# One edit to a fused audio tower on one core: taps and projection of the first image pair by tile, and eps inside the square

## The chip, the cores and the metric

The kernel runs on one core of a Trainium2 chip. The metric is the time of one execution on the device in microseconds. One execution was also recorded by the hardware profiler. Five engines appear in it: TensorE (PE; PEld is its weight load), VectorE (DVE), ScalarE (ACT), GpSimd (POOL), and SyncE (SP), which starts most of the DMAs. Each works through its own list of instructions in order, and semaphores tie the lists together.

## What is computed

The input `x` has 16 images of 64 channels by 250 tokens. Cut to what matters:

```python
x_sp = depthwise_conv(x, conv_w, K=3, pad=1) + conv_b        # (16, 64, 250)
x_mixed = swapaxes(x_sp, 1, 2) @ lin_w.T + lin_b + emb.mean(0)   # (16, 250, 128)
h = (x_mixed - mean) * rsqrt(var + 1e-5) * ln_g + ln_b
n = layernorm(h)
QK = (n @ WQ) @ (n @ WK).T
c0 = argmin(QK[0].sum(-1))
A = softmax(QK / 8); A[:, c0, :] = 0
h = h + A @ (n @ WV)
n = layernorm(h)
h = h + (gelu(n @ tril(W1).T + b1)) @ tril(W2).T + b2        # the FFN mixes along the 128 features
```

Everything is float32, except for the shift of the projection, which pairs 2 to 7 add as three bfloat16 parts.

## The kernel before, in words

Two images form a pair k (0 to 7): channels of one on partitions 0 to 63, of the other on 64 to 127, tokens along the free axis. An image's 250 tokens are split into two tiles of 125, the even ones (a = 0) and the odd ones (a = 1), so a pair has four tiles n = 2 * image + a.

**Front, per pair.** The three taps of the convolution are `first_tap` (ScalarE, line 479; for pair 0 it is `first_tap_0` on VectorE, line 629), `second_tap` and `third_tap` (VectorE, lines 634 and 644), each over 128 x 250. The result is `xc`. TensorE projects it with centred weights `lin_c` and adds the centred shift `cb_all`: `project_0_taps` and `project_0_bias` for pair 0 (lines 287 and 294), `project_1` (301), and `project(k)` for two pairs at a time (313). As weights and shift are centred over the 128 features, a row of the result has mean zero, and its variance is the mean of its squares. `square(k, n)` on ScalarE (line 529) squares a tile, scaled by 128 to the power -0.5, and sums the rows into `var_x`. `root_x` on GpSimd (line 189) raises it to -0.5. For pairs 0 and 1 eps comes in as a 129th column of the projection: `lin_c` has 0 there and `cb_all` has the square root of 128 eps (lines 780 and 781). For pairs 2 to 7 `root_x` adds eps in an operation of its own (line 194). `scale_x` (VectorE, 662) multiplies by this root and by gamma, and `head_h` (VectorE, pairs 0 and 1) or `add_beta` (GpSimd, 216) adds beta. Then `stats_1`, `aggregate_1`, `root_1` and `normalize_1` (or, for pairs 0 and 1, ScalarE's `normalize_tile` and `normalize_1_head`) make the normalized `n1`.

**Attention, per image b.** TensorE: `turn_n1` (349), `queries` (360), `scores` (366), `turn_a` (383), `mix` (395), `attend` (404). ScalarE carries each result out of PSUM: `out_n1t` (557), `out_p` (561), `exps` (567), `out_at` (575), `out_mix` (579). VectorE does `row_max` (709) and the residual. **FFN, per pair j.** `turn_n2`, `up`, `gelu`, `down`, `finish`.

The order of the work on each engine is written out by hand, at the foot of each block: lines 263 to 270 for GpSimd, 448 to 475 for TensorE, 598 to 621 for ScalarE, 785 to 813 for VectorE. `keep_warm` (274) issues multiplications whose results nobody reads. On ScalarE the pieces of the front lie between those of attention: the squares of pairs 2 and 3 are placed from line 601 to 603, those of pair 4 in line 605, of pair 5 in lines 606 and 607. GpSimd's operations have their operands in SBUF alone.

PSUM has eight banks. Pair 0's four tiles lie in `bank_x0` (image 0) and `bank_x1` (image 1). VectorE's first `scale_x(0, 0, 1)` waits for two squares and not one (line 664), since the second square reads the same bank.

Of the kernel before, what the change touches and what calls it, by code (L numbers as in the profile page):

```python
# [5 lines left out]
ALU = mybir.AluOpType  # L6
# [5 lines left out]
EPS = 1e-5  # L12
# [3 lines left out]
def audio_tower(nc, x, tok_pack, weights, rows, out):  # L16
# [4 lines left out]
    E = D + 1  # L21
# [8 lines left out]
    with ExitStack() as ctx:  # L30
# [6 lines left out]
        def bank(name):  # L37
# [5 lines left out]
        x0_ps = [t[0:H, 0:2 * E].rearrange("p (a d) -> p a d", a=2) for t in bank_x]  # L43
        x1_ps = [t[0:H, 0:2 * E].rearrange("p (a d) -> p a d", a=2) for t in bank_s]
# [23 lines left out]
        lin_c = sb("lin_c", [128, E])  # L68
# [3 lines left out]
        cb_all = sb("cb_all", [128, E])  # L72
        cb_all_2 = cb_all[:, :].unsqueeze(1).broadcast_to((128, 2, E))
# [28 lines left out]
        xc = [sb(f"xc{p}", [128, T]) for p in range(CONVS)]  # L102
        xc_halves = [t[:, :].rearrange("c (p a) -> c a p", a=2) for t in xc]
        squared = sb("squared", [H, NP, 4, E])
        var_x = sb("var_x", [H, NP, 4])
        var_x_eps = sb("var_x_eps", [H, NP, 4])
# [34 lines left out]
        ones_ready, iota_ready, tri_ready, mean_w_ready, warm_ready, columns_set = (  # L141
            sem(n) for n in ("ones_ready", "iota_ready", "tri_ready", "mean_w_ready", "warm_ready", "columns_set"))
# [3 lines left out]
        cb_mid_ready, cb_rest2_ready, cb_ready, below_ready, token_sum_ready, xvar_eps_ready = (  # L146
            sem(n) for n in ("cb_mid_ready", "cb_rest2_ready", "cb_ready", "below_ready", "token_sum_ready",
                             "xvar_eps_ready"))
        qk_mm, qk_copied, wv_mm, wv_ready, w1_mm, w1_ready = (
            sem(n) for n in ("qk_mm", "qk_copied", "wv_mm", "wv_ready", "w1_mm", "w1_ready"))  # L150
        tap0_0_ready = sem("tap0_0_ready")
# [121 lines left out]
        def _(pe):  # L273
# [13 lines left out]
            def project_0_taps():  # L287
                pe.wait_ge(lin_centred, 1)
                pe.wait_ge(conv_ready, 1)
                for a in range(2):  # L290
                    for place, half in halves(x0_ps):
                        nc.tensor.matmul(place[:, a, :], xc_halves[0][half, a, :], lin_c[half, :], start=(a == 0), stop=False)

            def project_0_bias():
                pe.wait_ge(row_pick_ready, 2)
                pe.wait_ge(cb_all_ready, 1)
                for place, half in halves(x0_ps):
                    nc.tensor.matmul(place, row_pick[half, 0:1].broadcast_to((C, H)), cb_all_2[half],
                                     start=False, stop=True).then_inc(x_mm, 1)

            def project_1():
                pe.wait_ge(conv_ready, 2)
                for place, half in halves(x1_ps):
                    nc.tensor.matmul(place, row_pick[half, 0:1].broadcast_to((C, H)), cb_all_2[half],
                                     start=True, stop=False)
                for a in range(2):
                    for place, half in halves(x1_ps):
                        last = nc.tensor.matmul(place[:, a, :], xc_halves[1][half, a, :], lin_c[half, :],
                                                start=False, stop=(a == 1))
                        if a == 1:  # L310
                            last.then_inc(x_mm, 1)

            def project(k):
                if k == 2:
                    pe.wait_ge(ones_ready, 1)
                    pe.wait_ge(cb_ready, 1)
                pe.wait_ge(conv_ready, k + 2)
                pe.wait_ge(x_scaled, 4 if k == 2 else 4 * k)
                for place, half in halves(x_two_ps):
                    nc.tensor.matmul(place, ones_b[half, :], cb_rows_4[half], start=True, stop=False)  # L320
                for q in range(2):
                    for a in range(2):
                        for place, half in halves(x_two_ps):
                            last = nc.tensor.matmul(place[:, q, a, :], xc_halves[(k + q) % CONVS][half, a, :], lin_c[half, 0:D],  # L324
                                                    start=False, stop=(q == 1 and a == 1))
                            if q == 1 and a == 1:
                                last.then_inc(x_mm, 1)
# [124 lines left out]
            keep_warm(2)  # L452
            project_0_taps(); project_0_bias()
# [24 lines left out]
        def _(act):  # L478
            def first_tap(k):
                if k == 1:  # L480
                    act.wait_ge(pads_zeroed, 2)
                act.wait_ge(landed_x[k], 16)
                if k >= 2:
                    act.wait_ge(tap01_ready, k - 1)
                nc.scalar.activation(tap0[k % 2][:, :], x_all[:, k, 0:T], ACT.Identity, scale=tok_w[:, D:D + 1],
                                     bias=conv_b).then_inc(tap0_ready, 1)

            def centre_lin():
                nc.scalar.activation(lin_scaled[:, :], lin_t, ACT.Identity, scale=-1.0 / D,
                                     accum_out=neg_lin_mean[:, :]).then_inc(lin_summed, 1)  # L490
                act.wait_ge(lin_summed, 1)
                act.wait_ge(columns_set, 1)
                nc.scalar.activation(lin_c[:, 0:D], lin_t, ACT.Identity, bias=neg_lin_mean[:, :]).then_inc(lin_centred, 1)

            def centre_bias():
# [4 lines left out]
                act.wait_ge(columns_set, 2)  # L500
                nc.scalar.activation(cb_all[:, 0:D], cb_ps, ACT.Identity, bias=neg_cb_mean[:, :]).then_inc(cb_all_ready, 1)

            def bias_hi():
                act.wait_ge(cb_all_ready, 1)
                nc.scalar.activation(cb_hi[:, :], cb_all[:, 0:D], ACT.Copy).then_inc(cb_hi_ready, 1)
# [122 lines left out]
        def _(dve):  # L628
            def first_tap_0():
                dve.wait_ge(landed_x[0], 16)  # L630
                nc.vector.tensor_scalar(tap0[0][:, :], x_all[:, 0, 0:T], tok_w[:, D:D + 1], conv_b,
                                        ALU.mult, ALU.add).then_inc(tap0_0_ready, 1)

            def second_tap(k):
                if k == 0:
                    dve.wait_ge(tap0_0_ready, 1)
                else:
                    dve.wait_ge(tap0_ready, k)
                if k >= 2:
                    dve.wait_ge(conv_ready, k - 1)  # L640
# [21 lines left out]
            def scale_x(k, first, m):  # L662
                dve.wait_ge(rstd_x_ready, 4 * k + first + m)
                if k == 0 and first + m == 1:
                    dve.wait_ge(xvar_ready, 2)
# [4 lines left out]
                for n in range(first, first + m):  # L670
                    x = (x0_ps, x1_ps)[k][n // 2][:, n % 2, 0:D] if k < 2 else x_two_ps[n // 2][:, k % 2, n % 2, :]
# [108 lines left out]
            nc.vector.memset(lin_c[:, D:E], 0.0).then_inc(columns_set, 1)  # L780
            nc.vector.memset(cb_all[:, D:E], (EPS * D) ** 0.5).then_inc(columns_set, 1)
# [3 lines left out]
            first_tap_0(); second_tap(0); third_tap(0); bias_rest(); second_tap(1); bias_rest2()  # L785
            third_tap(1)
# [55 lines left out]
```

## Time and profile before

| | |
|---|---|
| time, median of 3 runs | 94.32 us (94.21 to 94.5) |
| the profiled execution | 93.75 us; its span in the trace 92.0 us |
| TensorE (PE) busy | 85.0 us, 92% of the span, 541 instructions |
| VectorE busy | 73.6 us, 80%, 283 |
| ScalarE busy | 67.6 us, 73%, 241 |
| GpSimd busy | 54.9 us, 60%, 89 |
| granted TensorE clock | full in all 40 slices of the span |

Busy shares are means over stages with different limits: the front of the first pairs fills roughly the first 18 us, attention and the later pairs' fronts overlap until about 70, then comes the FFN. A row of the chain of waits has start, duration, engine and line, in time order. A row of the timeline has start, duration, engine, line, operation, output and inputs, shapes and how many instructions are merged in it; in brackets is the idle time before it and what ended it. Ends of matmuls are modelled, so consecutive groups on PE overlap slightly.

### The profile page before, as it was taken

The numbers are of one execution on the slowest core, as the hardware profiler recorded it, in microseconds if no ns is written. First come the engines' busy times: TensorE is split into PE (matmuls) and PEld (weight loads), VectorE is DVE, ScalarE is ACT, GpSimd is POOL, SyncE is SP. The second block draws the span as 40 slices with busy tenths as digits, with TensorE's granted clock in tenths as the row PEclk, the third lists the DMA queues.
The fourth block names the chain that finished last, engine by engine and source line by source line (L and its number), as shares of the span: only waits on it lengthen the run. The fifth ranks groups of instructions, "written<-read, shape, count | busy, mean of one in ns | idle before, by whom it ended". The sixth has DMA issues, their size and how long they took to land.

```text
span 92.0 us, 1984 instructions
## 1 busy us (share of the span) xinstructions
PE 85.0 (92%) x541; PEld 69.5 (76%) x541; DVE 73.6 (80%) x283; ACT 67.6 (73%) x241; POOL 54.9 (60%) x89
## 2 busy tenths in 40 slices
PE   5979987699999999999999999999999999999940
PEld 2446565379799989999899899989887988687730
DVE  2259999998999998999998899869769395862560
ACT  1688999999999769969787988666796735555400
POOL 5508768898856793999982079972708437460000
PEclk9999999999999999999999999999999999999999
DMA  1986000000000000000000000000000003425364
GB/s 23 218 289 200 0 0 4 4 0 0 11 0 0 0 0 0 0 7 4 4 0 0 0 0 7 0 0 0 0 0 0 0 7 111 115 69 154 108 188 150
DMA packets 3828, 3.84 MB, mean 42 GB/s; under 512 B 413, under 2 KB 3690, under 8 KB 3818
## 3 DMA queue, kind: packets, MB, share of 16 engines
q1 hardware_dynamic: 3466, 3.35, 13.1%
q10 hardware_dynamic: 352, 0.38, 1.4%
q8 instruction: 4, 0.07, 0.3%
q14 instruction: 6, 0.05, 0.2%
HBM read 1.68 MB, written 2.05 MB: 40 GB/s over the span
## 4 chain that ended last, share of the span: by engine, by line
PE 72%; DVE 8%; POOL 8%; DMA 3%; issue 3%; ACT 1%; POOLq 0%; DVEq 0%
PE bank_m L400 14%; PE bank_s L373 12%; PE bank_o L411 8%; PE bank_s L431 7%; PE bank_at L391 7%; PE bank_np L364 6%; PE bank_np L444 4%; PE bank_x L422 4%; POOL rstd L207 4%; DMA tok_w<-tok_dram 3%; PE bank_np L356 3%; PE bank_at L444 3%; POOL rstd_x L198 2%; DVE hb_all L774 2%; DVE bn L688 1%
## 5 line engine op out<-in xcount | busy, mean ns | idle before, releaser
L373 PE MATMUL bank_s<-n1t,pt 128*125 128x250 f32 x64 | 16.0, 375 | 0.5 <-ACT pt L565 0.5
L400 PE MATMUL bank_m<-at,n 125*128 125x250 f32 x64 | 16.2, 374 | 0.0
L570 ACT ACTIVATE a<-bank_s,neg_max 125x250 f32<-125x250 f32 x32 | 15.1, 479 | 0.7 <-DVE neg_max L711 0.7
L222 POOL TENSOR_TENSOR hb_all<-h_all,rows_sb 125x512 f32<-125x512 f32 x8 | 10.2, 1272 | 4.0 <-DVE h_all L747 4.0
L711 DVE TENSOR_REDUCE neg_max<-bank_s 125x2 f32<-125x500 f32 x16 | 10.7, 670 | 2.1 <-PE bank_s L373 2.1
L373 PEld LDWEIGHTS bank_s<-n1t,pt 128*125 128x125 f32 x64 | 11.0, 187 | 1.6 <-issue 0.6
L400 PEld LDWEIGHTS bank_m<-at,n 125*128 125x128 f32 x64 | 11.2, 190 | 0.9
L577 ACT ACTIVATE at<-bank_at 125x500 f32<-125x500 f32 x16 | 9.6, 597 | 1.9 <-PE bank_at L391 1.9
L207 POOL TENSOR_TENSOR rstd<-var_eps,neg_half 125x4 f32<-125x4 f32 (+2 forms) x11 | 9.5, 863 | 1.9 <-DVE var_eps L700 0.6
L364 PE MATMUL bank_np<-n1t,qk_w 128*128 128x250 f32 x32 | 9.6, 381 | 0.6 <-ACT n1t L559 0.6
L747 DVE SCALAR_TENSOR_TENSOR h_all<-bank_o,rinv_keep,h_all 125x128 f32<-125x128 f32 x32 | 9.6, 343 | 0.2
L391 PE MATMUL bank_at<-ident,a 125*125 125x125 f32 x64 | 9.7, 274 | 0.0
L411 PE MATMUL bank_o<-wv_c,mixed 128*125 128x128 f32 x64 | 9.6, 272 | 0.0
L411 PEld LDWEIGHTS bank_o<-wv_c,mixed 128*125 128x125 f32 x64 | 8.9, 187 | 0.8 <-issue 0.5
L391 PEld LDWEIGHTS bank_at<-ident,a 125*125 125x125 f32 x64 | 8.8, 188 | 0.9 <-issue 0.2
L214 POOL TENSOR_TENSOR rstd<-var_eps,neg_half 125x4 f32<-125x4 f32 x8 | 8.8, 1105 | 0.6
L565 ACT ACTIVATE pt<-bank_np 128x250 f32<-128x250 f32 x16 | 6.2, 385 | 3.2 <-PE bank_np L364 3.0
L581 ACT ACTIVATE mixed<-bank_m 128x250 f32<-128x250 f32 x16 | 6.1, 383 | 3.2 <-PE bank_m L400 3.2
L537 ACT ACTIVATE squared<-bank_x 125x128 f32<-125x128 f32 (+1 forms) x28 | 7.7, 293 | 0.9 <-PE bank_x L324 0.9
L218 POOL TENSOR_TENSOR h_all<-scaled,rows_sb 125x512 f32<-125x512 f32 x6 | 7.7, 1290 | 1.0 <-DVE scaled L672 1.0
L593 ACT ACTIVATE g<-bank_s,w_sb 128x500 f32<-128x500 f32 x8 | 5.3, 676 | 3.9 <-PE bank_s L431 3.3
L431 PE MATMUL bank_s<-n2t,w_c 128*128 128x500 f32 x16 | 8.0, 583 | 0.0
(121 smaller groups left out, 193.4 us busy)
## 6 DMA issues: line engine op xcount, KB each, us to landing
out_dram<-hb_all SPq DMA_DIRECT2D x7, 224.0 KB
x_all<-x_dram SPq DMA_DIRECT2D x8, 125.0 KB, 4.9
w_sb<-weights_dram SPq DMA_DIRECT2D x1, 320.5 KB, 5.7
out_dram<-hb_all SPq DMA_DIRECT2D x2, 112.0 KB
rows_sb<-rows_dram ACTq DMA_DIRECT2D x1, 187.5 KB
out_dram<-hb_all SPq DMA_DIRECT2D x6, 26.0 KB
tok_w<-tok_dram ACTq DMA_DIRECT2D x1, 130.0 KB, 3.1
out_dram<-hb_all ACTq DMA_DIRECT2D x2, 26.0 KB
```

Source lines behind the costliest of these rows:

```text
L207: pool.tensor_tensor(rstd1[:, k, tiles], var1_eps[:, k, tiles], neg_half[:, tiles], ALU.pow)\
L222: pool.tensor_tensor(hb_all[:, j, :, :], h_tiles[:, j, :, :], b2_4, ALU.add).then_inc(hb_ready, 1)
L364: nc.tensor.matmul(p_ps, qk_w[:, :], n1t[b % DEEP][:, :], start=True, stop=True).then_inc(p_mm, 1)
L373: last = nc.tensor.matmul(s_ps[b % 2][:, a, :], pt[b % DEEP][:, a * H:(a + 1) * H], n1t[b % DEEP][:, :], start=True, stop=True)
L391: last = nc.tensor.transpose(at_ps[:, c, a * H:(a + 1) * H], a_sb[b % DEEP][:, a, c * H:(c + 1) * H], ident[0:H, 0:H])
L400: last = nc.tensor.matmul(mix_ps, n1[b // 2 % (HELD // 2)][:, 2 * (b % 2) + c, :], at_sb[b % DEEP][:, c, :], start=(c == 0), stop=(c == 1))
L411: last = nc.tensor.matmul(o_ps[:, a, :], mixed[b % DEEP][:, a * H:(a + 1) * H], wv_c[:, :], start=True, stop=True)
L431: nc.tensor.matmul(f1_ps[j % 2], w1_c[:, :], n2t[j % 2][:, :], start=True, stop=True).then_inc(f1_mm, 1)
L570: ins = nc.scalar.activation(a_sb[b % DEEP][:, a, :], s_ps[b % 2][:, a, :], ACT.Exp, bias=neg_max[b % 2][:, a:a + 1], accum_out=exp_sum[:, ...
L577: nc.scalar.activation(at_sb[b % DEEP][:, :, :], at_ps, ACT.Copy).then_inc(at_ready, 1)
L711: nc.vector.tensor_reduce(neg_max[b % 2][:, :], s_ps[b % 2], AX_X, ALU.max, negate=True).then_inc(max_ready, 1)
L747: last = nc.vector.scalar_tensor_tensor(h, o_ps[:, a, :], rinv_keep[:, b // 2, n:n + 1], h, ALU.mult, ALU.add)
```

## The change

Five things are done.

1. `square` adds `root_eps`, a column of 125 partitions with the value (eps / 128) to the power 0.5, inside the square, for all pairs. The sum over a row of (x / sqrt(128) + sqrt(eps / 128)) squared is the variance plus eps, since the row's sum is zero.
2. With that the 129th column goes (`E = D + 1` becomes D all over) with its two memsets, and so do the six additions of eps in `root_x`. One memset of `root_eps` comes instead.
3. The three taps of pair 0 are done tile by tile: six VectorE operations over 128 x 125, which read `x_all` at every second element and write `xc` at every second one.
4. The projection of pair 0 is done tile by tile: taps and bias of tile a = 0 of both images, then those of a = 1. Tile (image 0, a = 1) gets a place in `bank_o`, so the two tiles of image 0 lie in banks of their own. `x_mm` rises after (image 0, a = 0), (image 0, a = 1) and (image 1, a = 1). The shift is added by four multiplications of 128 columns, before by two of 258. The wait of `scale_x(0, 0, 1)` for the second square goes. `w1_centre`, which uses `bank_o`, waits for two tiles of `x_scaled`.
5. One of the two `keep_warm` multiplications ahead of the projection of pair 0 goes.

The lists are otherwise in the same order. The diff, cut to its core (renumbered semaphore counts and the declarations are left out):

```diff
-        x0_ps = [t[0:H, 0:2 * E].rearrange("p (a d) -> p a d", a=2) for t in bank_x]
+        x0_ps = [[bank_x[0][0:H, 0:D], bank_o[0:H, 0:D]], [bank_x[1][0:H, 0:D], bank_x[1][0:H, D:2 * D]]]
...
             def root_x(k, first, m):
                 tiles, done = slice(first, first + m), 4 * k + first + m
                 pool.wait_ge(xvar_ready, done)
-                var = var_x
-                if k >= 2:
-                    pool.tensor_tensor(var_x_eps[:, k, tiles], var_x[:, k, tiles], eps[:, tiles], ALU.add)\
-                        .then_inc(xvar_eps_ready, 1)
-                    pool.wait_ge(xvar_eps_ready, k - 1)
-                    var = var_x_eps
-                pool.tensor_tensor(rstd_x[:, k, tiles], var[:, k, tiles], neg_half[:, tiles], ALU.pow).then_inc(rstd_x_ready, m)
+                pool.tensor_tensor(rstd_x[:, k, tiles], var_x[:, k, tiles], neg_half[:, tiles], ALU.pow).then_inc(rstd_x_ready, m)
...
-            def project_0_taps():
-                pe.wait_ge(lin_centred, 1)
+            def project_0_taps(a):
+                if a == 0:
+                    pe.wait_ge(lin_centred, 1)
+                pe.wait_ge(conv_0_ready, a + 1)
+                for par in range(2):
+                    half = slice(par * C, (par + 1) * C)
+                    nc.tensor.matmul(x0_ps[par][a], xc_halves[0][half, a, :], lin_c[half, :], start=True, stop=False)
+
+            def project_0_bias(a):
+                if a == 0:
+                    pe.wait_ge(row_pick_ready, 2)
+                    pe.wait_ge(cb_all_ready, 1)
+                for par in range(2):
+                    half = slice(par * C, (par + 1) * C)
+                    last = nc.tensor.matmul(x0_ps[par][a], row_pick[half, 0:1].broadcast_to((C, H)), cb_all[half, :],
+                                            start=False, stop=True)
+                    if par == 0 or a == 1:
+                        last.then_inc(x_mm, 1)
...
             def w1_centre():
                 pe.wait_ge(tri_ready, 2)
+                pe.wait_ge(x_scaled, 2)
                 nc.tensor.matmul(w1_ps, centre[:, :], w1_t, start=True, stop=True).then_inc(w1_mm, 1)
...
             bias_mean()
-            keep_warm(2)
-            project_0_taps(); project_0_bias()
+            keep_warm(1)
+            project_0_taps(0); project_0_bias(0); project_0_taps(1); project_0_bias(1)
             keep_warm(4)
...
             def square(k, n):
                 par, a = n // 2, n % 2
-                if k < 2:
-                    act.wait_ge(x_mm, 2 * k + par + 1)
-                    x, junk = (x0_ps, x1_ps)[k][par][:, a, :], squared[:, k, n, :]
+                if k == 0:
+                    act.wait_ge(root_eps_set, 1)
+                    act.wait_ge(x_mm, min(n + 1, 3))
+                    x = x0_ps[par][a]
+                elif k == 1:
+                    act.wait_ge(x_mm, 3 + par + 1)
+                    x = x1_ps[par][:, a, :]
                 else:
-                    act.wait_ge(x_mm, 4 + 2 * (k // 2 - 1) + par + 1)
-                    x, junk = x_two_ps[par][:, k % 2, a, :], squared[:, k, n, 0:D]
-                nc.scalar.activation(junk, x, ACT.Square, scale=float(D) ** -0.5,
+                    act.wait_ge(x_mm, 5 + 2 * (k // 2 - 1) + par + 1)
+                    x = x_two_ps[par][:, k % 2, a, :]
+                nc.scalar.activation(squared[:, k, n, :], x, ACT.Square, scale=float(D) ** -0.5, bias=root_eps[:, :],
                                      accum_out=var_x[:, k, n:n + 1]).then_inc(xvar_ready, 1)
...
-            def first_tap_0():
-                dve.wait_ge(landed_x[0], 16)
-                nc.vector.tensor_scalar(tap0[0][:, :], x_all[:, 0, 0:T], tok_w[:, D:D + 1], conv_b,
+            def x0_shifted(c):
+                return x_all[:, 0, c:c + T - 1:2]
+
+            def first_tap_0(a):
+                if a == 0:
+                    dve.wait_ge(landed_x[0], 16)
+                nc.vector.tensor_scalar(tap0_halves[:, a, :], x0_shifted(a), tok_w[:, D:D + 1], conv_b,
                                         ALU.mult, ALU.add).then_inc(tap0_0_ready, 1)
 
+            def second_tap_0(a):
+                dve.wait_ge(tap0_0_ready, a + 1)
+                nc.vector.scalar_tensor_tensor(tap01_halves[:, a, :], x0_shifted(a + 1), tok_w[:, D + 1:D + 2],
+                                               tap0_halves[:, a, :], ALU.mult, ALU.add).then_inc(tap01_0_ready, 1)
+
+            def third_tap_0(a):
+                dve.wait_ge(tap01_0_ready, a + 1)
+                nc.vector.scalar_tensor_tensor(xc_halves[0][:, a, :], x0_shifted(a + 2), tok_w[:, D + 2:D + 3],
+                                               tap01_halves[:, a, :], ALU.mult, ALU.add).then_inc(conv_0_ready, 1)
+
...
             def scale_x(k, first, m):
                 dve.wait_ge(rstd_x_ready, 4 * k + first + m)
-                if k == 0 and first + m == 1:
-                    dve.wait_ge(xvar_ready, 2)
...
-            nc.vector.memset(lin_c[:, D:E], 0.0).then_inc(columns_set, 1)
-            nc.vector.memset(cb_all[:, D:E], (EPS * D) ** 0.5).then_inc(columns_set, 1)
+            nc.vector.memset(root_eps[:, :], (EPS / D) ** 0.5).then_inc(root_eps_set, 1)
             nc.vector.memset(ones_b[:, :], 1.0).then_inc(ones_ready, 1)
             dve.wait_ge(pads_zeroed, 2)
             dve.wait_ge(landed_tok, 16)
-            first_tap_0(); second_tap(0); third_tap(0); bias_rest(); second_tap(1); bias_rest2()
-            third_tap(1)
+            first_tap_0(0); second_tap_0(0); third_tap_0(0); first_tap_0(1); second_tap_0(1)
+            third_tap_0(1); bias_rest(); second_tap(1); bias_rest2(); third_tap(1)
```

## Rows read from the trace of the kernel before

**Rows 1.** Chain of waits: start us, duration us, engine, line

```profile
24.17 0.70 DVE n L706
...
24.92 0.43 PE bank_np L356 x2
...
26.62 0.85 PE bank_m L400 x4
```

**Rows 2.** Busy time by stretch: us, then PE, PEld, DVE, ACT, POOL

```profile
9.20:18.30 9.10, 7.44 (x45) 4.86 (x44) 8.91 (x37) 8.92 (x44) 7.08 (x15) 1.00 0.01 2
24.92:87.40 62.48, 62.48 (x403) 54.66 (x403) 52.46 (x206) 46.39 (x151) 37.22 (x45) 1.00 0.08 22
```

**Rows 3.** Waits of PE from 9 to 18.5: total us, times, longest

```profile
PE bank_np L364 <- ACT n1t L559: 0.6, 1, 0.6
```

**Rows 4.** Timeline of PE: start us, duration us

```profile
6.09 0.63 PE L298 MATMUL bank_x<-cb_all,row_pick 64*125 64x258 f32 x4
...
20.55 0.43 PE L320 MATMUL bank_x<-cb_rows,ones_b 64*125 64x512 bf16 x2
...
23.80 1.01 PE L400 MATMUL bank_m<-at,n 125*128 125x250 f32 x4
...
26.04 0.58 PE L364 MATMUL bank_np<-n1t,qk_w 128*128 128x250 f32 x2
...
29.23 0.59 PE L364 MATMUL bank_np<-n1t,qk_w 128*128 128x250 f32 x2
...
38.60 0.59 PE L364 MATMUL bank_np<-n1t,qk_w 128*128 128x250 f32 x2
```

**Rows 5.** Timeline of ACT: start us, duration us

```profile
6.09 0.59 ACT L485 ACTIVATE tap<-x_all,tok_w 128x250 f32<-128x250 f32 x1 [0.36 <-DMA x_all<-x_dram]
...
9.24 0.28 ACT L537 ACTIVATE squared<-bank_s 125x129 f32<-125x129 f32 x1 [0.32 <-PE bank_s L308]
...
17.87 0.38 ACT L565 ACTIVATE pt<-bank_np 128x250 f32<-128x250 f32 x1
...
20.11 0.69 ACT L549 ACTIVATE n<-h_all,rstd 125x128 f32<-125x128 f32 x2 [0.21 <-POOL rstd L207]
...
25.39 0.38 ACT L559 ACTIVATE n1t<-bank_np 128x250 f32<-128x250 f32 x1
...
28.34 0.45 ACT L559 ACTIVATE n1t<-bank_np 128x250 f32<-128x250 f32 x1
...
37.95 0.39 ACT L559 ACTIVATE n1t<-bank_np 128x250 f32<-128x250 f32 x1
```

**Rows 6.** Groups of ACT by shape: count, busy us, mean ns, idle before

```profile
L570 ACT ACTIVATE a<-bank_s,neg_max 125x250 f32<-125x250 f32 x32 | 15.1, 479 | 0.7 <-DVE neg_max L711 0.7
...
L537 ACT ACTIVATE squared<-bank_x 125x128 f32<-125x128 f32 x24 | 6.7, 298 | 0.9 <-PE bank_x L324 0.9
...
L565 ACT ACTIVATE pt<-bank_np 128x250 f32<-128x250 f32 x16 | 6.2, 385 | 3.2 <-PE bank_np L364 3.0
...
L537 ACT ACTIVATE squared<-bank_x 125x129 f32<-125x129 f32 x4 | 1.0, 264 | 0.0
...
L501 ACT ACTIVATE cb_all<-bank_s,neg_cb_mean 128x128 f32<-128x128 f32 x1 | 0.4, 368 | 0.0
```

**Rows 7.** Timeline of DVE: start us, duration us

```profile
3.96 0.41 DVE L631 TENSOR_SCALAR tap<-x_all,tok_w 128x250 f32<-128x250 f32 x1 [2.33 <-DMA tok_w<-tok_dram]
...
4.92 0.48 DVE L648 SCALAR_TENSOR_TENSOR xc<-x_all,tok_w,tap 128x250 f32<-128x250 f32 x1
5.83 0.35 DVE L654 SCALAR_TENSOR_TENSOR cb_rest<-cb_hi,neg_below,cb_all 128x128 f32<-128x128 bf16 x1 [0.43 <-ACT cb_hi L505]
...
18.28 2.12 DVE L672 SCALAR_TENSOR_TENSOR scaled<-bank_x,rstd_x,rows_sb 125x128 f32<-125x128 f32 x8
...
21.35 0.87 DVE L688 BATCH_NORM_STATS2 bn<-h_all 125x6 f32<-125x128 f32 x4 [0.36 <-POOL h_all L218]
```

**Rows 8.** Instructions of line 194, POOL: duration ns min/median/max

```profile
L194 POOL TENSOR_TENSOR var_x_eps<-var_x,eps x6: 202/224/748, 16.2 to 42.7; 125x4 f32<-125x4 f32 x6
```

More of the change, by code:

```diff
@@ L71, in audio_tower @@
         mean_w = sb("mean_w", [128, 128])
-        cb_all = sb("cb_all", [128, E])
-        cb_all_2 = cb_all[:, :].unsqueeze(1).broadcast_to((128, 2, E))
+        cb_all = sb("cb_all", [128, D])
+        cb_all_2 = cb_all[:, :].unsqueeze(1).broadcast_to((128, 2, D))
         cb_hi, cb_mid, cb_rows = (sb(n, [128, D], BF16) for n in ("cb_hi", "cb_mid", "cb_rows"))
@@ L102, in audio_tower @@
         xc = [sb(f"xc{p}", [128, T]) for p in range(CONVS)]
+        tap0_halves, tap01_halves = (t[0][:, :].rearrange("c (a p) -> c a p", a=2) for t in (tap0, tap01))
         xc_halves = [t[:, :].rearrange("c (p a) -> c a p", a=2) for t in xc]
-        squared = sb("squared", [H, NP, 4, E])
+        squared = sb("squared", [H, NP, 4, D])
+        root_eps = sb("root_eps", [H, 1])
         var_x = sb("var_x", [H, NP, 4])
-        var_x_eps = sb("var_x_eps", [H, NP, 4])
         rstd_x = sb("rstd_x", [H, NP, 4])
@@ L140, in audio_tower @@
                              "row_pick_zeroed", "row_pick_ready"))
-        ones_ready, iota_ready, tri_ready, mean_w_ready, warm_ready, columns_set = (
-            sem(n) for n in ("ones_ready", "iota_ready", "tri_ready", "mean_w_ready", "warm_ready", "columns_set"))
+        ones_ready, iota_ready, tri_ready, mean_w_ready, warm_ready, root_eps_set = (
+            sem(n) for n in ("ones_ready", "iota_ready", "tri_ready", "mean_w_ready", "warm_ready", "root_eps_set"))
         lin_summed, lin_centred, cb_mm, cb_summed, cb_all_ready, cb_hi_ready, cb_rest_ready = (
@@ L285, in halves, with project_1 @@
                 return [(place[par], slice(par * C, (par + 1) * C)) for par in range(2)]
-            def project_0_taps():
-                pe.wait_ge(lin_centred, 1)
-                pe.wait_ge(conv_ready, 1)
[L290 to L302, printed above, removed]
+            def project_0_taps(a):
[15 more added lines that the diff above has]
+                        last.then_inc(x_mm, 1)
+            def project_1():
+                pe.wait_ge(conv_ready, 1)
                 for place, half in halves(x1_ps):
@@ L323, in project @@
                         for place, half in halves(x_two_ps):
-                            last = nc.tensor.matmul(place[:, q, a, :], xc_halves[(k + q) % CONVS][half, a, :], lin_c[half, 0:D],
+                            last = nc.tensor.matmul(place[:, q, a, :], xc_halves[(k + q) % CONVS][half, a, :], lin_c[half, :],
                                                     start=False, stop=(q == 1 and a == 1))
@@ L482, in first_tap @@
                 act.wait_ge(landed_x[k], 16)
[L483 to L484 removed]
+                if k == 2:
+                    act.wait_ge(tap01_0_ready, 2)
+                elif k >= 3:
+                    act.wait_ge(tap01_ready, k - 2)
                 nc.scalar.activation(tap0[k % 2][:, :], x_all[:, k, 0:T], ACT.Identity, scale=tok_w[:, D:D + 1],
@@ L491, in centre_lin @@
                 act.wait_ge(lin_summed, 1)
-                act.wait_ge(columns_set, 1)
-                nc.scalar.activation(lin_c[:, 0:D], lin_t, ACT.Identity, bias=neg_lin_mean[:, :]).then_inc(lin_centred, 1)
+                nc.scalar.activation(lin_c[:, :], lin_t, ACT.Identity, bias=neg_lin_mean[:, :]).then_inc(lin_centred, 1)
             def centre_bias():
@@ L499, in centre_bias @@
                 act.wait_ge(cb_summed, 1)
-                act.wait_ge(columns_set, 2)
-                nc.scalar.activation(cb_all[:, 0:D], cb_ps, ACT.Identity, bias=neg_cb_mean[:, :]).then_inc(cb_all_ready, 1)
+                nc.scalar.activation(cb_all[:, :], cb_ps, ACT.Identity, bias=neg_cb_mean[:, :]).then_inc(cb_all_ready, 1)
             def bias_hi():
                 act.wait_ge(cb_all_ready, 1)
-                nc.scalar.activation(cb_hi[:, :], cb_all[:, 0:D], ACT.Copy).then_inc(cb_hi_ready, 1)
+                nc.scalar.activation(cb_hi[:, :], cb_all[:, :], ACT.Copy).then_inc(cb_hi_ready, 1)
             def bias_mid():
@@ L653, in bias_rest @@
                 dve.wait_ge(cb_hi_ready, 1)
-                nc.vector.scalar_tensor_tensor(cb_rest[:, :], cb_hi[:, :], neg_below[0][:, :], cb_all[:, 0:D],
+                nc.vector.scalar_tensor_tensor(cb_rest[:, :], cb_hi[:, :], neg_below[0][:, :], cb_all[:, :],
                                                ALU.mult, ALU.add).then_inc(cb_rest_ready, 1)
```

31 lines of the change are left out of this document (14 added, 17 removed).

## The prediction

> **What bounds the kernel now.** I read the chain of waits first. It ends in one long stretch of TensorE: VectorE's normalization for pair 2 runs 24.17 to 24.87, TensorE starts image 4 at 24.92, and the chain doesn't leave TensorE until the last stores [rows 1]. The table of stretches says how dense that is: from 24.92 to 87.40 TensorE is busy 62.48 of 62.48 us [rows 2]. So the end of the kernel is the moment at which TensorE's solid stretch begins, plus 62.5 us that the change doesn't touch, plus any new hole that it tears in it.
>
> What sets the beginning? The same table for 9.20 to 18.30 shows TensorE at 7.44 of 9.10 us, ScalarE at 8.92 and VectorE at 8.91 [rows 2]. The view of waits lists what TensorE waited for there, and ScalarE ended each of it; the longest is 0.6 us for `n1t` [rows 3]. The reader is to see that in this stretch TensorE waits for ScalarE, and ScalarE waits for nothing. Its last idle piece is 0.32 us before the first square of pair 1 at 9.24; then it works without a hole until `out_p(1)` ends at 18.25 [rows 5], and TensorE goes on right behind it. The printed chain runs through GpSimd and VectorE instead, but has little room: the work ahead of image 4 on TensorE, four passes of `mix(0)` from 23.80 that take 0.85 to issue, would let it start at 24.65 [rows 1, 4]. The two routes differ by 0.27 us. A gain on the printed one is capped there; a loss on ScalarE's is paid nearly in full.
>
> **The change, part by part.**
>
> *eps inside the square.* All 32 squares get `bias=root_eps[:, :]`, a [125,1] operand in SBUF, where they had none. The algebra holds because a centred row sums to zero. The operand's price is the step on which the forecast rests. The trace has no square with such an operand, so I bound it by neighbours, all from PSUM. An exponential over 250 elements with a column as bias takes 479 ns, a copy over 250 without one 385: 94 apart. Over 128 elements, `cb_all` with a column takes 368 and the present squares 298: 70 apart [rows 6]. Lower bound 70 ns, and as upper bound 368 less 264 of the cheapest squares, 104 [rows 6]. Below nothing I exclude, since no row with a column is shorter than its like without. I take 94, from 32 and 16 instances. Dependent pieces follow one another closely on ScalarE, so I count it in full.
>
> The Trainium skill, ScalarE: Activation LUTs, section "What ACT_TABLE_LOAD costs", speaks against this change: each per-partition pointer operand adds about 93 ns to an ACTIVATE. By that rule the sum below is the same within 0.03 us, by the lowest row it is 0.5 us smaller. The same section has ACTIVATEs that overlap by about as much, which is why the rival in which nothing is paid is named below.
>
> *GpSimd's additions.* Six `var_x_eps` additions go, 224 ns median each and some 0.13 of waiting behind each [rows 8]: about 0.7 us ahead of `add_beta(2)`. VectorE waited 0.36 for that at 21.35 [rows 7]. VectorE frees at 20.99, so the gain is 0.36 on that route, and 0.27 on TensorE by the cap above. It is worth that only if ScalarE isn't later.
>
> *Taps of pair 0 by tile.* Three operations of 250 elements become six of 125. Before, the third ended at 5.40 (4.92 plus 0.48) [rows 7]. A 128-element form takes 0.35 [rows 7]. Tile 0 from 3.96 [rows 7]: 0.35, 0.35, 0.35 and two steps of 0.035 give 5.08, 0.32 earlier. Tile 1 follows: its first operation starts at about 5.00, and the same chain ends at 6.13, 0.73 later than before. The elements are now two apart; if that made a half cost as much as a whole, 0.48, tile 1 would end at about 6.8. I take the unstrided price and keep the other for the range. Behind it `bias_rest` moves from 5.83 to 6.05 and ends at 6.4, before ScalarE wants it at about 6.6, behind the tap of pair 1 that waited for its DMA until 6.09 and takes 0.59 [rows 5, 7]. Without that cover it would cost 0.2.
>
> Nobody gains from the early tile: ScalarE reaches the first square only at about 6.8, after that same tap, and the old bias product was complete at 6.72 [rows 4, 5]. The dropped wait of `scale_x(0, 0, 1)` is worth nothing for the same reason: VectorE waits for GpSimd's root of tile 0. TensorE finishes later. The bias pair took 0.63, of which 0.09 is drain; half of 0.54 goes to each tile's taps and each tile's bias. So 6.13, 0.15 to start and twice 0.27 give 6.82, against 6.09 plus 0.54, 6.63 (next start 6.65). That is +0.17 for what is queued behind: warm-up products, `qk_product`, `project_1`. One warm-up product less lies before the taps, in idle time: nothing. `project_1` then ends at 9.38. ScalarE, held 0.38 by pair 0's four squares, is free at 8.92 plus 0.38, 9.30. So the first square of pair 1 starts 0.17 late, at 9.41, and covers both.
>
> *Edits with one answer.* 129 columns become 128, one memset goes, `w1_centre` waits for `x_scaled` 2 (met 5 us earlier): nothing. The waits of `first_tap(2)` and `second_tap(2)` on the new semaphores are met by 6.2, 2 us ahead of their instructions: nothing.
>
> **The sum.**
> - Up to `out_p(1)`: 0.17 plus the twelve squares of pairs 1 to 3, 1.13: +1.30, for TensorE behind it too.
> - From there to 24.92 TensorE has slack that absorbs: about 0.22 before `project(4)` at 20.55, which waits for `scale_x(3)` to end at 20.40, 0.06 of small holes, and the 0.27 [rows 4, 7]. Image 4 starts +0.75.
> - ScalarE itself: 1.30 less the 0.21 it had waited for GpSimd at 20.11, plus 0.38 for pair 4's squares: +1.47. Its `out_n1t(4)`, 25.39 plus 0.38, ends at 27.24, and `queries(4)`, due at 26.04, starts 0.22 short of that shift: +1.25 [rows 4, 5].
> - Pair 5's squares: ScalarE +1.85 at `out_n1t(5)`, 28.34 plus 0.45; `queries(5)` at 29.23 has 0.39 of slack: +1.46 [rows 4, 5].
> - ScalarE then has idle time before pair 6 (it is busy 46.39 of 62.48 us [rows 2]) and falls back in step. Seven squares of pairs 6 and 7 stand ahead of `out_n1t(8)`, 0.66, less 0.1 of holes; that copy ended at 38.34 and `queries(8)` started at 38.60 [rows 4, 5]. About 0.2 of slack (0.05 is transit) leaves +0.35, of which I count 0.25, for holes under 0.15 us that no view lists.
>
> Total +1.7. Against the profiled execution's own 93.75 (span 92.0, 1.75 around it) that is 95.45. The median of the runs shown is 94.32, 0.57 above it, and the forecast is for the median: **96.0**.
>
> **The rivals.**
> 1. *Only the head counts.* ScalarE's slack swallows pairs 4 to 7, as its 46.39 of 62.48 us in the last stretch suggests [rows 2]. Then +0.75 remains, 95.1. Against it: the two copies named have 0.27 and 0.44 us of slack. Chance 0.15.
> 2. *Faster: GpSimd's route decides.* The column's 0.1 us hides in ScalarE's overlap between instructions. Then squares cost nothing, ScalarE is 0.17 late at 9.41, which the 0.28 of holes before 23.80 absorbs, and the removed additions bring 0.27: 94.05. It decides once a square costs less than about 0.03 us. Against it: the 94 ns between two groups that follow one another equally closely. Chance 0.07.
> 3. *The two cancel.* A square costs 0.03 to 0.05 and the gain is eaten: 94.3. Chance 0.06.
> 4. *Strided taps are dear.* Tile 1 is done 0.65 later still; `project_1` and ScalarE behind it move by about as much: 96.6. For it: no row has two-apart operands. Against: one element per step seems to be VectorE's pace already (0.13 for 122 elements more). Chance 0.12.
>
> **How the numbers follow.** The likeliest case has 0.60; its own range, from 70 to 104 ns a square, is 95.4 to 96.4. Taking in rival 1 below and rival 4 above, 94.9 to 96.8 leaves some 0.2 out. A measurement here tells 0.3%, 0.28 us, from no change. Rival 2 lies on that edge, half of it under: faster 0.06. Rival 3 and the rest: same 0.07. Slower: 0.87.
>
> **What would show it.** Squares of 125x128 at about 390 ns instead of 298, 32 of them; ScalarE's busy time up by 3 us. The first square of pair 1 at about 9.4, `out_p(1)` near 19.2 instead of 17.87, image 4 near 25.7. New idle time on TensorE between 9 and 30, ended by `n1t`. GpSimd without the additions, and no wait of VectorE for `h_all` at 21. Half taps of 0.35; 0.45 would speak for rival 4. I am wrong if the squares keep their 298 ns, or if they take 390 and TensorE's solid stretch still begins by 25.0: then ScalarE had room where I saw none.

## The result, and the profile after

The changed kernel takes 95.75 us (median of 4 runs, 95.32 to 96.94) against 94.26 for the kernel before (median of 4, 94.21 to 94.5). The ratio is 1.0137, with a 95% interval of 1.009 to 1.0185: slower by 1.3 us. The forecast was 96.0, with 94.9 to 96.8 as range. The profiled execution took 95.55 us, with a span of 93.8. Ratios leave disturbed executions out, here the one of 96.94 us (the median of the other three is 95.55), which is why an interval can be narrower than the spread of its runs.

The groups of ScalarE by shape hold the largest term, against [rows 6]:

```profile
L573 ACT ACTIVATE a<-bank_s,neg_max 125x250 f32<-125x250 f32 x32 | 15.6, 493 | 0.7 <-DVE neg_max L725 0.7
L540 ACT ACTIVATE squared<-bank_x,root_eps 125x128 f32<-125x128 f32 x27 | 10.3, 394 | 0.9 <-PE bank_x L322 0.9
...
L540 ACT ACTIVATE squared<-bank_s,root_eps 125x128 f32<-125x128 f32 x4 | 1.5, 365 | 0.3 <-PE bank_s L306 0.3
```

The name `root_eps` now stands among the inputs, and a square takes 394 ns where it took 298: 96 more, with 94 forecast. The page's first part says what that is over 32 squares, ScalarE from 67.6 to 70.2 us; GpSimd falls from 54.9 to 53.0, as its six additions are gone:

```profile
PE 86.1 (92%) x544; PEld 69.6 (74%) x544; DVE 74.6 (79%) x285; ACT 70.2 (75%) x241; POOL 53.0 (56%) x83
```

The timeline of ScalarE, against [rows 5]:

```profile
5.92 0.60 ACT L486 ACTIVATE tap<-x_all,tok_w 128x250 f32<-128x250 f32 x1 [0.35 <-DMA x_all<-x_dram]
...
9.46 0.37 ACT L540 ACTIVATE squared<-bank_s,root_eps 125x128 f32<-125x128 f32 x1 [0.32 <-PE bank_s L306]
...
19.17 0.38 ACT L568 ACTIVATE pt<-bank_np 128x250 f32<-128x250 f32 x1
...
25.62 0.40 ACT L568 ACTIVATE pt<-bank_np 128x250 f32<-128x250 f32 x1
26.80 0.42 ACT L562 ACTIVATE n1t<-bank_np 128x250 f32<-128x250 f32 x1
```

The first square of pair 1 starts at 9.46 (9.41 forecast), `out_p(1)` at 19.17, 1.30 late (1.30 forecast), `out_n1t(4)` at 26.80, 1.41 late (1.47). The idle piece that stood before 20.11 is gone. Whether the longer squares delay what follows them is seen at the second square of pair 1. Before, it starts 0.26 behind the first (9.24), and in the changed kernel 0.36 behind it (9.46):

```profile
9.50 0.27 ACT L537 ACTIVATE squared<-bank_s 125x129 f32<-125x129 f32 x1
...
9.82 0.36 ACT L540 ACTIVATE squared<-bank_s,root_eps 125x128 f32<-125x128 f32 x1
```

The timeline of VectorE has the third tap of each of pair 0's two tiles, 0.35 us over 125 elements two apart, against [rows 7]:

```profile
4.57 0.35 DVE L648 SCALAR_TENSOR_TENSOR xc<-x_all,tok_w,tap 128x125 f32<-128x125 f32 x1
...
5.60 0.35 DVE L648 SCALAR_TENSOR_TENSOR xc<-x_all,tok_w,tap 128x125 f32<-128x125 f32 x1
```

The timeline of TensorE from its first long wait on, against [rows 4]:

```profile
18.45 0.69 PE L363 MATMUL bank_np<-n1t,qk_w 128*128 128x250 f32 x2 [0.89 <-ACT n1t L562]
...
26.16 0.40 PE L355 MATMUL bank_np<-ident,n 125*128 125x125 f32 x2 [0.16 <-ACT pt L568]
...
27.27 0.69 PE L363 MATMUL bank_np<-n1t,qk_w 128*128 128x250 f32 x2
...
30.65 0.69 PE L363 MATMUL bank_np<-n1t,qk_w 128*128 128x250 f32 x2
...
40.59 0.69 PE L363 MATMUL bank_np<-n1t,qk_w 128*128 128x250 f32 x2
```

`queries(4)` is 1.23 late (1.25 forecast), `queries(5)` 1.42 (1.46), `queries(8)` 1.99 (1.7). The table of stretches gives TensorE more idle time ahead of its solid stretch (6.79 busy of 9.10 us, before 7.44). The solid stretch itself starts 1.24 later and is also longer, 63.30 us for the same 403 instructions that took 62.48 [rows 2]:

```profile
9.20:18.30 9.10, 6.79 (x44) 4.24 (x42) 8.35 (x33) 8.73 (x40) 6.73 (x13) 1.00 0.01 2
26.16:89.46 63.30, 63.30 (x403) 54.40 (x403) 52.32 (x204) 47.51 (x152) 35.48 (x42) 1.00 0.07 21
```

That both rows read fully busy, though one took 0.82 longer, fits the modelled ends of matmuls, which can cover short stops. The chain of waits has such stops at `queries`, which waits for ScalarE's copy `n1t`. For image 4 this copy now ends at 27.22 and `queries` starts at 27.27; before it was 25.77 and 26.04. `queries` takes 0.42 us of the chain in the kernel before:

```profile
26.20 0.42 PE bank_np L364 x2
```

and in the changed kernel, for images 4, 5 and 8:

```profile
27.41 0.55 PE bank_np L363 x2
...
30.74 0.60 PE bank_np L363 x2
...
40.64 0.65 PE bank_np L363 x2
```

Ahead of that the chain has changed hands. It now leads through squares, where it led through GpSimd and VectorE [rows 1]. At its start it has the load of the weights, `w_sb`, for whose landing TensorE waits 0.18 us before `qk_product` at 7.88; this matters below:

```profile
1.72 6.03 DMA w_sb<-weights_dram
...
14.39 1.14 ACT squared L540 x6
15.80 0.70 ACT squared L540 x4
16.50 0.58 ACT n L552 x2
17.07 1.05 ACT squared L540 x6
...
23.77 1.01 ACT squared L540 x5
24.80 0.47 ACT squared L540 x2
```

### The profile page after: what moved, and what is told of

Read it like the earlier page. It is cut to its first block, busy times and chain, and to the rows that moved or that the text cites. A ratio compares the mean times of both kernels' runs of the same rounds, so it can differ in the third digit from the quotient of the medians.

```text
span 93.8 us, 1989 instructions
## 1 busy us (share of the span) xinstructions
PE 86.1 (92%) x544; PEld 69.6 (74%) x544; DVE 74.6 (79%) x285; ACT 70.2 (75%) x241; POOL 53.0 (56%) x83
## 4 chain that ended last, share of the span: by engine, by line
PE 76%; ACT 8%; DMA 6%; DVE 4%; issue 1%; SPq 1%; DVEq 0%
PE bank_m L399 14%; PE bank_s L372 13%; PE bank_o L410 7%; PE bank_np L363 7%; PE bank_at L390 7%; PE bank_s L430 7%; DMA w_sb<-weights_dram 6%; ACT squared L540 5%; PE bank_np L355 4%; PE bank_np L443 4%; PE bank_x L421 4%; PE bank_x L322 3%; PE bank_at L443 3%; DVE hb_all L788 1%; PE bank_x L318 1%
## 5 line engine op out<-in xcount | busy, mean ns | idle before, releaser
L573 ACT ACTIVATE a<-bank_s,neg_max 125x250 f32<-125x250 f32 x32 | 15.6, 493 | 0.7 <-DVE neg_max L725 0.7
L191 POOL TENSOR_TENSOR rstd_x<-var_x,neg_half 125x4 f32<-125x4 f32 (+2 forms) x11 | 10.1, 924 | 8.1 <-ACT squared L540 8.1
L540 ACT ACTIVATE squared<-bank_x,root_eps 125x128 f32<-125x128 f32 x27 | 10.3, 394 | 0.9 <-PE bank_x L322 0.9
L686 DVE SCALAR_TENSOR_TENSOR scaled<-bank_x,rstd_x,rows_sb 125x128 f32<-125x128 f32 x27 | 7.5, 340 | 0.9 <-ACT squared L540 0.7
```

Of the source, the lines that this page charges most:

```text
L191: pool.tensor_tensor(rstd_x[:, k, tiles], var_x[:, k, tiles], neg_half[:, tiles], ALU.pow).then_inc(rstd_x_ready, m)
L540: nc.scalar.activation(squared[:, k, n, :], x, ACT.Square, scale=float(D) ** -0.5, bias=root_eps[:, :], accum_out=var_x[:, k, n:n + 1]).th ...
L573: ins = nc.scalar.activation(a_sb[b % DEEP][:, a, :], s_ps[b % 2][:, a, :], ACT.Exp, bias=neg_max[b % 2][:, a:a + 1], accum_out=exp_sum[:, ...
```

## The experiments

**Which part costs: the column or the tiles?** Four kernels cross the two. The first takes the column out of the changed kernel (ScalarE's group is shown behind the result):

```diff
-                nc.scalar.activation(squared[:, k, n, :], x, ACT.Square, scale=float(D) ** -0.5, bias=root_eps[:, :],
+                nc.scalar.activation(squared[:, k, n, :], x, ACT.Square, scale=float(D) ** -0.5, bias=(EPS / D) ** 0.5,
```

> The changed kernel with one edit: the squares' bias is a number in the instruction and not a column in SBUF. Theory (the column's price on ScalarE's path is the whole loss): squares of 125x128 back from 394 to about 298 ns, the first square of pair 1 at about 9.4, out_p(1) near 18.0, time 94.0 (93.8 to 94.3), as GpSimd's removed additions can now bring up to 0.27 and pair 0's tiles take up to 0.17. Rival (tiling pair 0 delays TensorE and with it all): stays above 95.2.

Measured: 94.15 us, ratio to the kernel before 0.9969 (0.9946 to 0.9992).

```profile
L540 ACT ACTIVATE squared<-bank_x 125x128 f32<-125x128 f32 x27 | 7.7, 300 | 1.0 <-PE bank_x L322 0.9
```

The square is back at 300 ns, and the rival about tiles falls: with the tiles in and the column out, the whole loss is gone. From ScalarE's timeline of this kernel: the first square of pair 1 starts at 9.47, against 9.46 with the column, but `out_p(1)` at 18.15, against 19.17:

```profile
9.47 0.28 ACT L540 ACTIVATE squared<-bank_s 125x128 f32<-125x128 f32 x1 [0.32 <-PE bank_s L306]
...
18.15 0.38 ACT L568 ACTIVATE pt<-bank_np 128x250 f32<-128x250 f32 x1
```

The second puts the column alone into the kernel before (its 129th column and GpSimd's additions out, taps and projection of pair 0 untouched):

```diff
-                nc.scalar.activation(junk, x, ACT.Square, scale=float(D) ** -0.5,
+                nc.scalar.activation(junk, x, ACT.Square, scale=float(D) ** -0.5, bias=root_eps[:, :],
```

> The kernel before with the column alone: eps inside the square as a column, no 129th column, no additions of GpSimd; taps and projection of pair 0, the warm-up and the wait for the second square as before. Theory: 95.5 (95.2 to 95.8), squares at 390 ns; within 0.2 of the changed kernel. Rival (pair 0's tiles are the cause): 94.3.

Measured: 95.65 us, ratio 1.0137 (1.0105 to 1.0168), the changed kernel's own. The third is the same with the number in place of the column.

> The kernel before with eps inside the square as a number in the instruction, no 129th column and no additions of GpSimd; pair 0 as before. Theory: squares at 298 ns, VectorE's wait for h_all at 21 gone, time 94.0, up to 0.27 below the kernel before and not more, since TensorE's own work ahead of image 4 ends at 24.65. Rival (GpSimd's additions were hidden): 94.3, as before.

Measured: 93.67 us, ratio 0.9934 (0.9909 to 0.9958). It beats both kernels: 0.6 us under the one before, 1.9 under the changed one. Against `old_col`, from which it differs in the operand of the squares alone, it is 2.0 us faster: that is the column's price with nothing else changed. VectorE's wait for `h_all` is gone, as expected. The gain over the kernel before is larger than the 0.27 that theory allowed, and the profile doesn't show where it lies: `queries(8)` starts at 38.59, in the profile of before at 38.60 [rows 4], though that profile was a quick execution (below). Two more kernels price the additions. One has tiles, the number for pairs 0 and 1, and GpSimd's additions for the others:

```diff
+                if k >= 2:
+                    pool.tensor_tensor(var_x_eps[:, k, tiles], var_x[:, k, tiles], eps[:, tiles], ALU.add)\
+                        .then_inc(xvar_eps_ready, 1)
```

> Pair 0 by tile as in the changed kernel, eps as a number in the squares of pairs 0 and 1, and GpSimd's six additions for pairs 2 to 7 back. Theory: squares at 298 ns, pair 0's tiles cost TensorE 0.17 at 9.2 and ScalarE as much, most of it absorbed or paid behind the GpSimd route: 94.3 to 94.5. Against tiles_imm this prices the additions (0.2 to 0.3 less there). Rival (tiles are a gain): below 94.1.

Measured: 94.36 us, ratio 1.001 (0.9991 to 1.0029); against 0.9969 that makes the additions worth 0.4 us. The other is the kernel before without the additions and with nothing in their place.

> The kernel before without GpSimd's six additions and nothing else changed. It leaves eps out for pairs 2 to 7. Theory (capped by TensorE's own work ahead of image 4): 0.1 to 0.3 under the kernel before, 94.0 to 94.2. Rival (the whole gain of old_imm, 0.6, is the additions'): 93.7.

Measured: 93.97 us, ratio 0.997 (0.9953 to 0.9987): 0.3 us. The cap of 0.27 is within the uncertainty of both. The rest of `old_imm`'s 0.6, some 0.3, is not clear of noise (its interval and that of `no_adds` overlap). It could belong to the 129th column and its two memsets, but no run isolates them, and the traces don't speak for it: from the first square of pair 1 to `queries(8)` pass 29.33 us in `old_imm` and 29.21 in `no_adds`, which has the 129th column. It stays open. The tiles (with the dropped warm-up product), `tiles_imm` against `old_imm`, cost 0.0035 or 0.3 us with the number, where the two intervals overlap as well, and nothing that can be told with the column (1.0137 both).

**Where does ScalarE's time count?** The changed kernel with the column for one half of the pairs and the number for the other:

```diff
-                nc.scalar.activation(squared[:, k, n, :], x, ACT.Square, scale=float(D) ** -0.5, bias=root_eps[:, :],
+                nc.scalar.activation(squared[:, k, n, :], x, ACT.Square, scale=float(D) ** -0.5,
+                                     bias=root_eps[:, :] if k < 4 else (EPS / D) ** 0.5,
```

> The changed kernel with the column in the squares of pairs 0 to 3 alone; pairs 4 to 7 take the number. Theory (every square that stands ahead of a late copy on ScalarE pays): image 4 on TensorE near 25.8 as in the changed kernel, no further loss later: 0.8 to 1.1 over the kernel with the number everywhere (94.15), so 95.0 to 95.25. Rival (only the head counts): as the changed kernel, 95.7.

> The changed kernel with the column in the squares of pairs 4 to 7 alone; pairs 0 to 3 take the number. Theory: queries(4) 0.2 to 0.35 late, queries(5) 0.3 more, queries(8) 0.3 more: 0.6 to 1.0 over 94.15, so 94.75 to 95.15, and the two halves together give the changed kernel's 1.6. Rival (only the head counts, ScalarE's idle time after 30 us swallows these): 94.15.

Measured: 94.73 (ratio 1.0038, 1.0016 to 1.006) and 94.93 (1.007, 1.0047 to 1.0093). Against 0.9969 the halves cost 0.0069 and 0.0101, or 0.65 and 0.95 us, together 0.0170; the changed kernel's step over `tiles_imm` is 0.0168. The later half is within what was expected, the head below its 0.8 to 1.1. The rival that only the head counts falls: the later half costs about as much. TensorE's timeline of `col_head`, `queries(4)` and `queries(8)`:

```profile
27.03 0.69 PE L363 MATMUL bank_np<-n1t,qk_w 128*128 128x250 f32 x2
...
39.70 0.59 PE L363 MATMUL bank_np<-n1t,qk_w 128*128 128x250 f32 x2
```

and of `col_late`:

```profile
26.41 0.68 PE L363 MATMUL bank_np<-n1t,qk_w 128*128 128x250 f32 x2
...
39.72 0.69 PE L363 MATMUL bank_np<-n1t,qk_w 128*128 128x250 f32 x2
```

In `tiles_imm` the same two start at 26.07 and 38.73. With the column in the head 0.96 is lost by `queries(4)` (0.11 of it already stands at the first square of pair 1, 9.58 against 9.47), and 0.97 by `queries(8)`: nothing more. With the column in the late pairs it is 0.34 and then 0.99. So pairs 4 to 7 lose 0.65 between these two points in a stretch where ScalarE has idle time on the whole. The chain of `col_late` has the same short stops as the changed kernel: `queries` takes 0.60 at 29.86 and 0.65 at 39.77, where an undelayed one takes 0.42. So ScalarE's idle pieces lie elsewhere than the copies for which TensorE stops.

**Twice the suspected cost.** The scale goes in as a second column:

```diff
-                nc.scalar.activation(squared[:, k, n, :], x, ACT.Square, scale=float(D) ** -0.5, bias=root_eps[:, :],
+                nc.scalar.activation(squared[:, k, n, :], x, ACT.Square, scale=root_d[:, :], bias=root_eps[:, :],
```

> The changed kernel with the scale of all squares as a second column of SBUF (same value). Theory (each column operand costs ScalarE about 94 ns and the slack is used up already): squares at about 487 ns, time 97.3 to 97.9. Rival (the first operand is dear, a second one is free, or the loss saturates): below 96.2.

Measured: 100.38 us, median of four between 98.3 and 101.07, no ratio. The operand behaves as expected, 480 ns, 86 more:

```profile
L541 ACT ACTIVATE squared<-bank_x,root_eps,root_d 125x128 f32<-125x128 f32 x27 | 12.7, 480 | 0.9 <-PE bank_x L323 0.9
```

The time doesn't: 4.6 us over the changed kernel where 1.6 to 2.2 were expected. The table of stretches of its profiled execution (us, then PE, PEld, DVE, ACT, POOL busy, the granted clock, the DMA share and GB/s) shows the rest:

```profile
17.00:18.00 1.00, 0.71 (x4) 0.30 (x4) 0.39 (x2) 1.00 (x5) 1.00 (x2) 1.00 0.00 0
18.00:19.00 1.00, 0.35 (x2) 0.11 (x2) 1.00 (x4) 1.00 (x6) 0.19 (x1) 0.85 0.02 8
19.00:20.00 1.00, 0.49 (x1) 0.50 (x2) 1.00 (x6) 1.00 (x6) 0.68 (x1) 0.50 0.00 0
...
25.00:26.00 1.00, 1.00 (x11) 0.74 (x12) 0.86 (x7) 0.75 (x4) 0.20 (x1) 0.74 0.00 0
26.00:27.00 1.00, 1.00 (x17) 0.88 (x14) 0.42 (x1) 0.62 (x4) 0.98 (x1) 1.00 0.00 0
```

TensorE's timeline of the same execution:

```profile
16.55 1.08 PE L373 MATMUL bank_s<-n1t,pt 128*125 128x250 f32 x4 [1.04 <-ACT pt L569]
17.91 0.43 PE L356 MATMUL bank_np<-ident,n 125*128 125x125 f32 x2 [0.29 <-ACT n L553]
19.50 1.20 PE L364 MATMUL bank_np<-n1t,qk_w 128*128 128x250 f32 x2 [1.16 <-ACT n1t L563]
...
21.75 1.87 PE L373 MATMUL bank_s<-n1t,pt 128*125 128x250 f32 x4
```

TensorE waits 1.04, 0.29 and 1.16 us within four microseconds. About 0.4 us into the third wait, at 18.7, the granted clock falls to 0.50, its lower level of 1.2 GHz, and it stays there until 25.5. Four passes of `scores` take 1.87 us there and 1.08 at 16.55. To part the two causes I filled the idle time with work for nothing. It is legal since `bank_at` is free between `out_wv` and `turn_a(0)`:

```diff
+            def keep_warm_at(count):
+                pe.wait_ge(wv_ready, 1)
+                for _ in range(count):
+                    nc.tensor.matmul(bank_at[0:64, :], warm[:, :], warm[:, :].unsqueeze(1).broadcast_to((128, 8, 64)),
+                                     start=True, stop=True)
...
-            turn_n1_tile(0); turn_n1_tile(1); project(2); queries(0); w1_centre(); scores(0); turn_n1(1)
-            queries(1); row_sums(); turn_n1(2); scores(1); turn_a(0); queries(2); project(4); turn_n1(3)
+            turn_n1_tile(0); turn_n1_tile(1); project(2); queries(0); w1_centre(); keep_warm_at(3); scores(0); keep_warm_at(1); turn_n1(1)
+            keep_warm_at(4); queries(1); row_sums(); turn_n1(2); scores(1); turn_a(0); queries(2); project(4); turn_n1(3)
```

> The kernel with two columns (100.38) and eight more multiplications whose results nobody reads, placed on TensorE where it idles between 15 and 19.5 us. Theory (of the 4.6 us between one column and two, some 1.7 are ScalarE's and some 3 are TensorE at the lower of its two levels from 18.9 to 25.3 us): granted clock 0.99 or more, four passes of scores(1) back from 1.87 to about 1.0, time 97.2 to 97.9, although work was added. Rival (the loss is ScalarE's alone, the clock goes with it): 100 or more.

Measured: 98.58 us, ratio 1.0447 (1.0412 to 1.0482), granted clock 0.991 to 0.996 in four of four. Its table of stretches:

```profile
14.00:19.00 5.00, 4.73 (x34) 2.93 (x31) 4.32 (x17) 4.97 (x22) 3.12 (x5) 1.00 0.02 5
19.00:25.00 6.00, 5.68 (x41) 4.17 (x40) 5.53 (x25) 5.90 (x23) 4.85 (x7) 1.00 0.01 1
```

and, from its timeline, the four passes that took 1.87:

```profile
21.30 1.01 PE L379 MATMUL bank_s<-n1t,pt 128*125 128x250 f32 x4
```

The median is 1.8 us lower with eight multiplications more. Three of `col_two`'s four executions had a mean clock of 0.966 to 0.983, and the one at 0.992 took 98.3, as `two_warm` does. So of the 4.6 us some 1.8 are the clock and 2.8 to 3.0 the operand, which is above the 97.2 to 97.9 expected. My size for the operand, 1.7, was too low. 32 squares at 86 ns are 2.8: that fits a second column paid in full, the slack having been used up by the first.

**How far two executions differ.** The kernel before, unchanged, once more.

> The kernel before once more, for a second profile of it: the first one took 93.75, 0.57 under the median. Theory (the difference between executions lies in when the loads land): tok_w, the x of pair 1 or w_sb land 0.1 to 0.4 us later than in the first profile and everything after is shifted by as much. Rival: the front is the same to 0.05 us and the difference lies in the last stores.

Measured: 94.25 us, first square of pair 1 at 9.73 and not 9.24. Two of the three loads named weren't late: VectorE's first tap, behind `tok_w`, starts at 3.82 against 3.96, and the tap of pair 1 at 5.80 against 6.09. The third was. TensorE's timeline of the execution of [rows 4] has:

```profile
4.01 0.46 PE L282 MATMUL bank_s<-tok_w,mean_w 128*128 128x128 f32 x2
...
7.63 0.49 PE L332 MATMUL bank_m<-w_sb 128*128 128x128 f32 x2
```

and that of this one:

```profile
3.95 0.80 PE L282 MATMUL bank_s<-tok_w,mean_w 128*128 128x128 f32 x2
...
8.16 0.46 PE L332 MATMUL bank_m<-w_sb 128*128 128x128 f32 x2 [0.22 <-DMA w_sb<-weights_dram]
```

Two things differ here: the product of shift and means takes 0.80 us where it took 0.46, and `qk_product` waits for `w_sb`. The other profiles part them. Here are four of the kernels with the time that the profile gives `w_sb` from issue to landing, and the starts of `qk_product` and of the first square of pair 1:

| | product at 4.0 | `w_sb` lands | `qk_product` | first square of pair 1 |
|---|---|---|---|---|
| `before` | 0.46 | 5.7 us | 7.63 | 9.24 |
| `old_imm` | 0.80 | 5.8 us | 7.68 | 9.26 |
| `before_2` | 0.80 | 6.3 us | 8.16 | 9.73 |
| `two_warm` | 0.46 | 6.3 us | 8.15 | 9.73 |

The square follows `w_sb` and not the slow product. In all twelve profiles it starts 1.57 to 1.61 us after `qk_product`, and a later landing never goes with an earlier square. So the theory holds for one load, `w_sb`, at 0.6 us and not 0.1 to 0.4. The 0.5 us of the front go through to the end (93.75 and 94.25).

## Why the prediction was right

- *The stretch that sets the start.* TensorE waits for ScalarE, and ScalarE for nothing: shown. Without the column `out_p(1)` moves from 19.17 to 18.15, with the first square of pair 1 in the same place (9.46 and 9.47), and the loss is gone. One wait of TensorE in the changed kernel, 0.77 us before `scores(0)`, is put down to VectorE's `scaled`, which ended at 15.88; ScalarE's copy `pt`, which it needs too, had ended 0.08 before. In `old_col` the same wait is `pt`'s.
- *94 ns a square, of 70 to 104.* Measured 96 (394 less 298), and 94 against `tiles_imm` (300). An exponential and a copy over 250 elements gave it, which differ in their function as well, so that it came this close is in part luck; the nearer shape, `cb_all`, would have given 70. By the rule of the Trainium skill, ScalarE: Activation LUTs, "What ACT_TABLE_LOAD costs", each pointer operand adds about 93 ns; this case's rows agree, 96 for the first and 86 for the second.
- *Nothing hides it.* The second square of pair 1 starts 0.36 behind the first and not 0.26, in `col_two` 0.45: the operand isn't covered by the overlap between instructions. `out_p(1)`, `queries(4)` and `queries(5)` came within 0.05 us of the working.
- *The first square of pair 1, +0.17: the number was luck.* It came at 9.46, 0.22 late, but the four warm-up products behind pair 0's projection start at 6.65 in both profiles. What held `qk_product`, and with it `project_1` and the square, is the wait for `w_sb` (6.0 us to landing against 5.7), which differs between executions of one kernel and which the working didn't have. Measured from the square on, `out_p(1)` is 1.08 late (1.13 forecast) and `queries(8)` 1.77 (1.53).
- *Image 4, +0.75: wrong.* One wait was left out. TensorE started it 1.24 late, because `turn_n1(4)` also waits for `out_p(3)` (25.62 plus 0.40), which I hadn't listed. It made no difference to the sum, as `queries(4)` was to be held for the same shift by `out_n1t(4)`.
- *Pairs 6 and 7, 0.25.* Too small: from `queries(5)` to `queries(8)` the lateness grew from 1.42 to 1.99, by 0.57. In the times the whole step is smaller, 1.3 us by the ratio, in `old_col` too, so the sum of 1.7 was high by 0.4 there. The profiles of before and after are 1.8 apart, but that of before is an execution in which `w_sb` landed early, 0.5 under the second one. Against the median of all four, 95.75, the forecast of 96.0 is 0.25 high, and against 95.55 it is 0.45; both lie inside the range.
- *GpSimd's additions, up to 0.27 and worth nothing behind the column.* Shown by `tiles_adds` and `no_adds`: 0.3 to 0.4 without the column. That with the column the gain is covered is argued from the chain; no run has the column and the additions.
- *Tiles, 0.17 late on TensorE, nothing gained.* The half taps took 0.35, as assumed, so elements two apart cost VectorE nothing that shows, and rival 4 falls. TensorE's tile 1 started 0.40 after VectorE's last tap had started, at 6.00. From VectorE's first tap to the warm-up products behind the projection pass 2.85 us (3.80 to 6.65), before 2.69 (3.96 to 6.65): 0.16 more, as worked out. It doesn't show in the starts, as VectorE began 0.16 earlier in this execution, and the wait for `w_sb` would have covered it. Without the column the tiles cost 0.3 us in the ratios, at the edge of what these can tell.
- *Rival 1* falls with `col_late`, *rivals 2 and 3* with the 394 ns and the 0.36 from one square to the next.

## What to carry to other kernels

A per-partition column as bias or scale cost ScalarE about 0.09 us in each square here, 0.10 for the first column and 0.09 for the second from one square to the next. When the value is the same on all partitions, write it as a number: the algebra of eps inside the square was worth 0.6 us here, and the column turned that into a loss of 1.3. An engine's idle share over a long stretch says little about slack, and a fully busy one may hide short stops: compare each result that another engine waits for with the moment it was wanted. And where squares or copies stand in front of such a result, every 0.09 us counts. Before you put a shift in the front of a profile down to the change, look for a load that landed at another time.

## What the runs showed of the hardware that was not expected

TensorE's clock makes a small delay large. In `col_two`, waits of 1.04 and 0.29 us and 0.4 us of a third, all between 15.5 and 18.7 us, were followed by 6.8 us at a granted clock of 0.50, some 1.8 us of loss, and with eight multiplications in the idle time no such loss showed in four executions of four. The changed kernel has part of that idle time (waits of 0.77 and 0.89 us in the same place). Its profiled clock was still full there, but its execution of 96.94 us had a mean clock of 0.975, and two of `col_head`'s twelve had 0.978 and 0.979, while no execution of the kernel before with a clock on record is under 0.992. Where in those three the clock fell is not on record.

The load of the weights sets the front, and it varies. Issued at 1.7 us in each profile, `w_sb` landed 5.7 us later in one execution of the kernel before and 6.3 in another, and the whole time moved by 0.5 us with it. The product at 4.0 us took 0.46 or 0.80, while the rows give the granted clock as 1.00 in both; why is not shown, and neither the first square of pair 1 nor the time followed it. A single profile is no measure of a change of 0.3 us.
